# Causal latent attention: the mask added by a TensorE product before the exponential, in place of GpSimd selects and keep-busy products

## The chip, the cores and the metric

One Trainium2 chip, one core of it. The metric is device time of one execution in microseconds (us), the median of several runs. TensorE is the matrix engine (PE in the profile, PEld its weight loads), VectorE is DVE, ScalarE is ACT, GpSimd is POOL, SyncE is SP.

## The reference, cut to what matters

The whole kernel is a stack of four layers of gated attention and feed-forward blocks on x of shape (8, 256, 128). The changed part is the causal latent attention of layer 1. Per batch b of 8, with 16 heads of width 8 and T = 256 rows:

```
x = rmsnorm(x)
q = (x @ Wq.T);  latent = layernorm(x @ Wdkv.T)
k = latent @ Wuk.T;  v = latent @ Wuv.T
q, k = apply_rope(q), apply_rope(k)
scores = einsum('bhqd,bhkd->bhqk', q, k) / sqrt(8)
scores = where(causal, scores, -inf)
attn = softmax(scores);  out = einsum('bhqk,bhkd->bhqd', attn, v) @ Wo.T
```

`causal` lets query i see the keys 0 to i.

## The kernel before, in words

All of the stage is in `latent_attention_layer` (line 1622). Each engine runs its own program; all walk the same list of **slots** (`slots(4)`, line 347): 16 slots n = 0 to 15 per batch b, one head per slot, from b = -4 to the batch after the last. What a slot holds besides its head is written out by hand as `if n == ... and alive(b + ...)`. So in one slot the engines work on the head of batch b, on the maxima of a head six slots ahead (`scored`, line 353), on the output of batch b - 1 and on the preparation of batches b + 1 to b + 4. Engines meet by semaphores only, and each engine keeps the order of its program: a wait holds everything behind it.

The main chain of a head: TensorE computes the scores twice, once with queries on the partitions for the maxima (line 1901) and once transposed, keys on the partitions (line 1907). Both are products over 32 rows, on row strips `head_strip(m)` and `head_strip(n)` (line 488), two per kind. VectorE takes the masked maxima of the first (line 1799, two passes a head, each with a short read of the accumulator), ScalarE takes the exponential of the second into the tile of probabilities (line 1839). Both kinds of scores have two PSUM banks, so TensorE may be two heads ahead of either engine, no more. The maxima of a whole batch go, split in three bf16 parts, into extra columns of the queries (`place_max`, lines 1781 to 1791, four short VectorE operations, each waiting for the one before), and the queries are turned again (line 1976), so that the score product subtracts the maximum by itself.

The exponentials of keys later than the query are not wanted. Before, GpSimd sets them to zero afterwards: `hide_later` (line 1716) runs two `affine_select` (line 1722) for every four heads, four slots after their group began, and signals `masked`. The mix of the probabilities with the values (`mix_group`, lines 1912 to 1926, 16 products) waits for that and stands in slots 9, 13, 1 and 5.

Other steps of a batch, by slot on TensorE: 0 turn of the normalised rows (1939) and of half 0 of the output of batch b - 1 (1990, `pe_turn_out_half`, products of line 565); 3 query and latent projection (1947) and turn of the queries (1954); 7 turn of the keys; 9 turn of half 1 of the output; 10 turn of the latent rows (1965); 12 turn of the attention output (1970) and of the queries with their maxima; 13 key/value product (1980); 15 output product (1986). In slots 1, 2, 10 and 11 two further products each, `pe_keep_busy` (line 585, product of line 588: 128 rows, 512 columns, bf16), write to a bank that nothing reads. VectorE: sum into the result in slot 0 (1805), which frees the output bank for the mix of slot 1; normalisation of an output half in slots 1 and 10 (`dve_normalise_half`, lines 575 and 580); row statistics 2, latent statistics 4, copy of the turned queries 5 (480), latent rows 8, placing of the maxima 9, copy 13 (485). ScalarE: expansions 0 and 2 (1832), copies 1, 6, 8, 11, copy of the output 13 (1874), of keys and values 14 (1867, 1870), of an output half 6 and 14 (557). GpSimd: selects 0, 4, 8, 12; low parts 1 and 3; latent scale 5; rows 6 (1666); rotation of the queries 9 and of the keys 14 (1704 to 1708); root mean square 13.

## Time and profile before

| | us |
|---|---|
| median of 3 runs | 1438.57 (1437.09 to 1443.74) |
| the profiled execution, its own time | 1453.79 |
| its span | 1452.0 |
| TensorE, VectorE, ScalarE, GpSimd busy | 1257.5, 828.2, 640.0, 615.5 |
| the attention of the change, from its first instruction to its last | 515.3 to 704.8 |
| granted TensorE clock, mean over the span | 0.912 of full |

The table is read from the head of the page and the timeline. The profiled execution is some 1% longer than the median. "Idle before" in a row is the time in which the engine had nothing to do, and behind the arrow stands what ended it.

### The profile page before, as it was taken

How to read it: one execution, taken by the hardware profiler on the slowest of the kernel's cores; microseconds unless marked ns; L12 is line 12 of the kernel's file. 1: busy time of each engine (PE TensorE's matmuls, PEld its weight loads, DVE VectorE, ACT ScalarE, POOL GpSimd, SP SyncE). 2: the span in 40 equal slices, each digit the busy share in tenths (PEclk: the TensorE clock that was granted, in tenths of full speed). 3: DMA queues.
4: the chain of work that ended last, by engine and by line, in shares of the span. 5: the costliest groups of instructions: out<-in, count | busy, mean ns of one | idle time of the engine just before them, and what ended most of it. 6: DMA issues, size and time to landing. Idle time of an engine off the chain costs nothing.

```text
span 1452.0 us, 26160 instructions
## 1 busy us (share of the span) xinstructions
PE 1257.5 (87%) x9483; PEld 864.9 (60%) x9483; DVE 828.2 (57%) x2599; ACT 640.0 (44%) x1310; POOL 615.5 (42%) x1162
## 2 busy tenths in 40 slices
PE   6999844799999938888799989988989899989897
PEld 3444323357778723444588944444877576878786
DVE  5568487455544237886266667873555443355554
ACT  1457634355554323666322227765223464232322
POOL 4234174675763276884334434533233783000000
PEclk9999956599999955999899969998999999899999
DMA  4400000000000000000000000001200000000001
GB/s 130 138 1 2 2 1 0 1 1 1 2 1 1 1 0 1 2 2 2 1 0 0 1 1 2 2 2 33 97 0 1 1 1 1 1 1 0 0 0 30
DMA packets 15337, 16.85 MB, mean 12 GB/s; under 512 B 6403, under 2 KB 12565, under 8 KB 14583
## 3 DMA queue, kind: packets, MB, share of 16 engines
q1 hardware_dynamic: 15222, 15.34, 3.4%
q8 instruction: 70, 1.15, 0.3%
q14 instruction: 45, 0.36, 0.1%
HBM read 14.28 MB, written 1.05 MB: 11 GB/s over the span
## 4 chain that ended last, share of the span: by engine, by line
PE 35%; DVE 6%; POOL 5%; issue 3%; ACT 2%; DVEq 0%; POOLq 0%; ACTq 0%
PE banks L3056 6%; PE banks L2446 4%; PE banks L3064 4%; PE banks L2194 3%; PE banks L2472 2%; PE banks L2810 2%; PE banks L2184 2%; PE banks L511 1%; PE banks L2781 1%; PE banks L550 1%; PE banks L2795 1%; PE banks L2857 1%; DVE x_resident L2137 1%; DVE f_hiddenT L2997 1%; PE banks L2455 1%
## 5 line engine op out<-in xcount | busy, mean ns | idle before, releaser
L525 DVE TENSOR_REDUCE x_minus_max<-banks 128x2 f32<-128x512 f32 x256 | 170.3, 687 | 68.7 <-PE banks L511 67.3
L533 ACT ACTIVATE x_probs<-banks 128x512 f32<-128x512 f32 x256 | 151.5, 600 | 102.8 <-PE banks L517 101.8
L511 PE MATMUL banks<-x_kT,x_qT 32*128 32x256 bf16 x512 | 108.3, 317 | 18.7 <-DVE x_minus_max L525 10.3
L3056 PE MATMUL banks<-xnT,w_f_w 128*128 128x256 f32 x512 | 119.8, 379 | 0.0
L517 PE MATMUL banks<-x_qT,x_kT 32*128 32x256 bf16 x512 | 102.8, 301 | 2.4 <-ACT x_probs L533 1.9
L3056 PEld LDWEIGHTS banks<-xnT,w_f_w 128*128 128x128 f32 x512 | 93.0, 190 | 10.3
L3031 ACT ACTIVATE f_gate<-banks 128x512 f32<-128x512 f32 x64 | 38.2, 597 | 127.6 <-PE banks L3056 127.6
L1799 DVE CUSTOM_DVE_ANT_0 f_masked_scores<-banks,hide_later_keys 128x128 f32<-128x128 f32 (+1 forms) x256 | 77.6, 352 | 28.1 <-PE banks L1901 27.1
L2997 DVE TENSOR_TENSOR f_hiddenT<-banks,f_gate 128x512 f32<-128x512 f32 x64 | 44.0, 689 | 70.8 <-ACT f_gate L3031 70.4
L511 PEld LDWEIGHTS banks<-x_kT,x_qT 32*128 32x128 bf16 x512 | 28.9, 96 | 90.8 <-DVE x_minus_max L525 50.6
L3064 PE MATMUL banks<-w_f_w,f_hiddenT 128*128 128x128 f32 x512 | 69.6, 279 | 15.1 <-DVE f_hiddenT L2997 15.1
L1839 ACT ACTIVATE f_probs<-banks 128x384 f32<-128x384 f32 x128 | 61.5, 497 | 47.5 <-PE banks L1907 47.0
L550 PE MATMUL banks<-x_probs,x_v_with_ones 128*32 128x256 f32 x1024 | 78.9, 433 | 0.4 <-ACT x_probs L533 0.4
L3064 PEld LDWEIGHTS banks<-w_f_w,f_hiddenT 128*128 128x128 f32 x512 | 64.9, 191 | 21.3 <-DVE f_hiddenT L2997 19.5
L1215 DVE TENSOR_REDUCE x_minus_max<-banks 128x2 f32<-128x512 f32 x64 | 43.3, 687 | 58.9 <-PE banks L1472 58.9
L222 POOL TENSOR_TENSOR ln_var_eps<-ln_mean_var,eps_1e 128x2 f32<-128x2 f32 x8 | 1.6, 197 | 173.6 <-DVE ln_mean_var L202 173.6
L2194 PE MATMUL banks<-w_f_w,m_hiddenT 128*128 128x128 f32 x512 | 63.7, 281 | 4.0 <-DVE m_hiddenT L2125 4.0
L2155 ACT ACTIVATE m_hiddenT<-banks,w_f_b 128x256 f32<-128x256 f32 x64 | 26.9, 471 | 89.2 <-PE banks L2184 89.2
L2194 PEld LDWEIGHTS banks<-w_f_w,m_hiddenT 128*128 128x128 f32 x512 | 60.8, 196 | 6.7 <-ACT m_hiddenT L2155 6.6
L1502 PEld LDWEIGHTS banks<-x_v_with_one,x_probs 128*128 128x128 f32 x512 | 60.3, 192 | 5.6 <-issue 5.6
L2184 PE MATMUL banks<-m_rowsT,w_f_w 128*128 128x256 f32 x256 | 61.7, 391 | 0.0
L1502 PE MATMUL banks<-x_v_with_one,x_probs 128*128 128x65 f32 x512 | 61.0, 273 | 0.0
(514 smaller groups left out, 3109.9 us busy)
## 6 DMA issues: line engine op xcount, KB each, us to landing
w_f_w<-in_f_w SPq DMA_DIRECT2D x5, 1024.0 KB, 6.9
out<-x_resident SPq DMA_DIRECT2D x1, 1024.0 KB, 5.1
x_resident<-in_x SPq DMA_DIRECT2D x1, 896.0 KB, 6.4
context_rows<-in_ctx SPq DMA_DIRECT2D x1, 768.0 KB, 4.9
contextT<-in_ctxT SPq DMA_DIRECT2D x1, 672.0 KB, 8.7
w_f_wg<-in_f_wg SPq DMA_DIRECT2D x1, 544.0 KB, 4.9
w_f_wu<-in_f_wu SPq DMA_DIRECT2D x1, 544.0 KB, 5.8
w_f_wd<-in_f_wd SPq DMA_DIRECT2D x1, 512.0 KB, 6.4
```

Of the source, the lines that this page charges most:

```text
L511: mm = nc.tensor.matmul(K.PS[:, SMAX0 + m % 2, t * S:(t + 1) * S], h["qT"][r, c % 3, g, t * P:(t + 1) * P], h["kT"][r, c % 3, g, :], start ...
L517: mm = nc.tensor.matmul(K.PS[:, ST0 + n % 2, t * S:(t + 1) * S], h["kT"][r, b % 3, g, t * P:(t + 1) * P], h["qT"][r, b % 3, g, :], start=T ...
L525: K.nc.vector.tensor_reduce(h["nm"][:, b % 2, :, n], K.PS[:, SMAX0 + n % 2, :].rearrange("p (t n) -> p t n", t=T), AX_X, ALU.max, negate=T ...
L533: K.nc.scalar.activation(h["p"][:, n % (2 * HG)], K.PS[:, ST0 + n % 2, :], ACT.Exp).then_inc(s["p"].sem, 1)
L550: mm = nc.tensor.matmul(K.PS[E * j:E * (j + 1), OUT0 + g // 2, (g % 2) * S:(g % 2 + 1) * S], h["ve"][:, b % 3, kt * H + n, :], h["p"][:, n ...
L1502: mm = nc.tensor.matmul(K.PS[:, OUT0 + t, at:at + V1], p[:, (2 * c + j) % 4, kt * S + t * P:kt * S + (t + 1) * P], ve[:, b % 2, kt, 2 * c ...
L1799: ins = nc.vector.tensor_tensor_reduce(unused[:, m % 2, t, 0:w], K.PS[:, SMAX0 + m % 2, t * P:t * P + w], hide[:, t, 0:w], -1.0, -HIDE, AL ...
L1839: nc.scalar.activation(h["p"][:, (b * H + n) % PROBS], K.PS[:, ST0 + n % 2, 0:WIDE], ACT.Exp).then_inc(s["p"].sem, 1)
L2184: mm = nc.tensor.matmul(K.PS[:, 2 * (e % 2) + c // 2, (c % 2) * S:(c % 2 + 1) * S], W["f1_w1"][:, (e * CE1 + c) * P:(e * CE1 + c + 1) * P] ...
L2194: mm = nc.tensor.matmul(K.PS[:, OUT0 + e % 2, t * D:(t + 1) * D], hT[:, e % 2, c, t * P:(t + 1) * P], W["f1_w2"][:, (e * CE1 + c) * D:(e * ...
L3056: mm = nc.tensor.matmul(K.PS[:, 2 * (e % 2) + k, c * S:(c + 1) * S], W[name][:, e * HE3 + c * P:e * HE3 + (c + 1) * P], K.norm["xnT"][:, u ...
L3064: mm = nc.tensor.matmul(K.PS[:, OUT0 + e % 2, t * D:(t + 1) * D], hT[:, e % 2, c, t * P:(t + 1) * P], W["f3_w2"][:, (e * CE3 + c) * D:(e * ...
```

## The change

The mask becomes a summand of the scores. For each head a product of the constant tile `hidden` (-1e30 where the key is later than the query, 0 elsewhere, in bf16, 128 x 128) with the identity, broadcast to both diagonal blocks, opens the accumulation of the score bank (256 columns, all 128 rows), and the two score products of line 1907 add to it. The exponential gives zero there by itself. GpSimd's selects and their semaphore are gone, and so are the eight keep-busy products of a batch. The mix waits for the exponentials. Several steps change slot: half 0 of the output turn from 0 to 2 and its normalisation from 1 to 3, turn of the queries 3 to 4, half 1 of the output turn 9 to 8 and its normalisation 10 to 9, attention output turn 12 to 11 and its copy 13 to 12, key/value product 13 to 14 with its copies and the rotation of the keys 14 to 15. `place_max` is a generator, whose four operations are spread: at the ends of slots 9 and 10, and between the two passes of the maxima in slots 10 and 11.

```diff
 def causal_mixed_at(b, n):
-    i = b * H + n - MASKED_SLOT
+    i = b * H + n - MIXED_LATE
...
@@ gpsimd
-                def hide_later(b, g):
-                    first = (b * G + g) % 3 * HG
-                    pool.wait_ge(s["p"].sem, s["p"].after(b, HG * (g + 1)))
-                    for kt in range(T):
-                        d = h["p"][:, first:first + HG, kt * S:kt * S + P]
-                        ins = nc.gpsimd.affine_select(d, d, pattern=[[0, HG], [1, P]], compare_op=ALU.is_ge, fill=0.0, base=0, channel_multiplier=-1)
-                    ins.then_inc(s["masked"].sem, 1)
...
-                    if n == 14 and alive(b + 3):
+                    if n == 15 and alive(b + 3):
                         rotate(b + 3, 1, s["k_read"], "ks", W["f1_rope"][:].rearrange("p (a t e) -> p a t e", a=2, t=T), s["rolled_k"])
@@ vector
+                nc.vector.tensor_copy(hidden[:], hide[:, 0, 0:P]).then_inc(ready.sem, 1)
...
                     nc.vector.tensor_copy(qe[:, :, :, 24], m).then_inc(steps.sem, 1)
-                    dve.wait_ge(steps.sem, steps.next())
+                    got = steps.next()
+                    yield
+                    dve.wait_ge(steps.sem, got)
                     nc.vector.tensor_tensor(h["nr"][:], m, qe[:, :, :, 24], ALU.subtract).then_inc(steps.sem, 1)
...
                         for t in range(T):
+                            if placing is not None and (n, t) in ((10, 1), (11, 1)):
+                                next(placing)
...
-                    if n == 1 and alive(b - 1):
+                    if n == 3 and alive(b - 1):
                         dve_normalise_half(K, dve, steps, s, h, b - 1, 0, None)
...
-                    if n == 9 and alive(b + 1):
-                        place_max(b + 1)
-                    if n == 10 and alive(b - 1):
+                    if n == 9 and alive(b - 1):
                         dve_normalise_half(K, dve, steps, s, h, b - 1, 1, None)
+                    if n == 9:
+                        placing = place_max(b + 1) if alive(b + 1) else None
+                    if n in (9, 10) and placing is not None:
+                        next(placing)
@@ tensor
+                    if alive(b):
+                        nc.tensor.matmul(K.PS[:, ST0 + n % 2, :].rearrange("p (t n) -> p t n", t=T)[:, :, 0:P], hidden[:],
+                                         K.identb[:].unsqueeze(1).broadcast_to([P, T, P]), start=True, stop=False, skip_group_check=True)
...
                             mm = nc.tensor.matmul(K.PS[:, ST0 + n % 2, t * S:t * S + (T - t) * P], h["kT"][r, b % 3, g, t * P:(t + 1) * P],
-                                                  h["qT"][r, b % 3, g, t * P:S], start=True, stop=True)
+                                                  h["qT"][r, b % 3, g, t * P:S], start=False, stop=True, skip_group_check=True)
...
                 def mix_group(b, g):
-                    pe.wait_ge(s["masked"].sem, s["masked"].after(b, g + 1))
+                    pe.wait_ge(s["p"].sem, s["p"].after(b, HG * (g + 1)))
...
-                    if n == 13 and alive(c):
+                    if n == 14 and alive(c):
                         pe.wait_ge(s["latT"].sem, s["latT"].after(c))
...
-                    if n == 0 and alive(b - 1):
+                    if n == 2 and alive(b - 1):
                         pe_turn_out_half(K, pe, s, h, b - 1, 0)
-                    if alive(b):
-                        last, before = min(c, B - 1), min(c - 1, B - 1)
-                        if n in (1, 2):
-                            pe.wait_ge(s["v"].sem, s["v"].after(before))
-                            pe.wait_ge(s["k_read"].sem, s["k_read"].after(before))
-                            pe_keep_busy(K, h, b, MISC)
-                            pe_keep_busy(K, h, b, MISC)
-                        if n in (10, 11):
-                            pe.wait_ge(s["lat"].sem, s["lat"].after(last))
-                            pe.wait_ge(s["q_read"].sem, s["q_read"].after(last))
-                            pe_keep_busy(K, h, b, MISC + 1)
-                            pe_keep_busy(K, h, b, MISC + 1)
```

The other slot changes are of the same form.

## Rows read from the trace of the kernel before

**Rows 1.** The page: TensorE's granted clock in 40 equal slices of the span

```profile
PEclk9999956599999955999899969998999999899999
```

**Rows 2.** Windows: length, PE PEld DVE ACT POOL busy (count), clock, DMA, GB/s

```profile
564.20:584.32 20.12, 17.65 (x144) 8.25 (x145) 14.94 (x84) 11.72 (x27) 14.35 (x30) 0.65 0.01 2
602.24:620.16 17.92, 15.75 (x188) 8.48 (x188) 15.17 (x86) 12.18 (x30) 15.75 (x33) 1.00 0.01 1
638.10:656.66 18.56, 16.67 (x185) 8.89 (x184) 14.70 (x82) 12.02 (x29) 12.06 (x25) 0.91 0.01 2
656.66:671.08 14.42, 13.25 (x176) 6.77 (x176) 12.14 (x72) 10.37 (x24) 7.55 (x14) 1.00 0.01 2
671.08:685.30 14.22, 12.13 (x146) 5.89 (x145) 9.18 (x51) 8.56 (x21) 4.90 (x8) 1.00 0.01 1
685.30:699.00 13.70, 11.70 (x126) 5.47 (x127) 1.66 (x6) 8.68 (x20) 5.34 (x9) 1.00 0.00 1
```

**Rows 3.** Timeline of TensorE, slot 13 to slot 3: start, us, engine, line, operation

```profile
615.86 0.23 PE L1901 MATMUL banks<-f_kT,f_qT 32*128 32x128 bf16 x1
...
616.92 1.13 PE L1980 MATMUL banks<-f_w_k_v,f_latT 128*128 128x256 f32 x4
...
617.98 0.23 PE L1901 MATMUL banks<-f_kT,f_qT 32*128 32x128 bf16 x1
...
618.00 0.22 PE L1901 MATMUL banks<-f_kT,f_qT 32*128 32x128 bf16 x1
...
619.05 0.09 PEld L1901 LDWEIGHTS banks<-f_kT,f_qT 32*128 32x128 bf16 x1 [0.27 <-DVE f_minus_max L1799]
...
619.32 0.44 PE L1939 MATMUL banks<-identity,y_resident 128*128 128x128 f32 x2
...
619.97 0.65 PE L565 MATMUL banks<-identity,f_outT 128*128 128x128 f32 x4 [0.21 <-ACT f_outT L557]
...
620.56 0.22 PE L1901 MATMUL banks<-f_kT,f_qT 32*128 32x128 bf16 x1
...
622.16 0.22 PE L1901 MATMUL banks<-f_kT,f_qT 32*128 32x128 bf16 x1
...
622.43 0.60 PE L588 MATMUL banks<-f_kT 128*128 128x512 bf16 x2
...
622.96 0.23 PE L1901 MATMUL banks<-f_kT,f_qT 32*128 32x128 bf16 x1
```

**Rows 4.** Timeline of VectorE and GpSimd, slots 9 to 11, and VectorE's wait in slot 4

```profile
612.07 0.35 DVE L1785 CAST f_q_expanded<-f_minus_max 128x32 bf16<-128x32 f32 x1
...
612.65 1.23 POOL L1722 TENSOR_SCALAR_AFFINE_SELECT f_probs<-f_probs 128x512 f32<-128x512 f32 x2
...
612.70 0.68 DVE L1789 CAST f_q_expanded<-f_minus_max_rest 128x32 bf16<-128x32 f32 x1
...
613.86 0.28 DVE L1799 CUSTOM_DVE_ANT_0 f_masked_scores<-banks,hide_later_keys 128x128 f32<-128x128 f32 x1
...
614.42 0.25 DVE L575 RECIPROCAL f_inverse_sums<-banks 128x16 f32<-128x16 f32 x1
...
614.70 0.29 DVE L580 TENSOR_TENSOR f_attention_out<-banks,f_inverse_sums 128x128 f32<-128x128 f32 x1
...
624.90 0.29 DVE L1799 CUSTOM_DVE_ANT_0 f_masked_scores<-banks,hide_later_keys 128x128 f32<-128x128 f32 x1 [0.52 <-PE banks L1901]
```

**Rows 5.** Timeline: the same cast beside a rotation step, and alone in batch 5

```profile
648.61 0.72 POOL L1708 TENSOR_TENSOR f_q_rows<-f_turned_a,f_turned_b 128x256 f32<-128x256 f32 x1
648.63 0.79 DVE L1789 CAST f_q_expanded<-f_minus_max_rest 128x32 bf16<-128x32 f32 x1
...
665.62 0.24 DVE L1789 CAST f_q_expanded<-f_minus_max_rest 128x32 bf16<-128x32 f32 x1
```

**Rows 6.** A window with the clock down in batch 4; timeline: the last mix

```profile
648.00:649.00 1.00, 1.00 (x8) 0.72 (x4) 0.93 (x3) 0.00 (x0) 0.92 (x3) 0.50 0.00 0
...
699.84 0.59 PEld L1923 LDWEIGHTS banks<-f_probs,f_v_with_ones 128*32 128x32 f32 x16 [0.50 <-POOL f_probs L1722]
```

More of the change, by code:

```diff
@@ L1602 @@
 LAT = 64
-MASKED_SLOT = 9
-def masked_at(b, n):
-    i = b * H + n - HG
-    if i % HG == 0 and alive(i // H):
-        return i // H, (i % H) // HG
-    return None
+MIXED_LATE = 9
 def causal_mixed_at(b, n):
-    i = b * H + n - MASKED_SLOT
+    i = b * H + n - MIXED_LATE
     if i % HG == 0 and alive(i // H):
@@ L1628, in latent_attention_layer @@
         s[extra] = K.rising("signal_" + extra, 1)
-    s["masked"] = K.rising("signal_masked", G)
     WIDE = S + P
@@ L1645, in latent_attention_layer @@
         hide = K.hide_q
-        ready = K.once("layer_setup_step", 2)
+        hidden = sb("hide_later_bf16", [P, P], BF16)
+        ready = K.once("layer_setup_step", 3)
         cleared = K.once("heads_values_cleared", 1)
@@ L1727, in _ @@
                 for b, n in slots(4):
-                    group = masked_at(b, n)
-                    if group:
-                        hide_later(*group)
                     if n == 1 and alive(b + 2):
@@ L1785, in place_max @@
                     nc.vector.tensor_copy(qe[:, :, :, 24], m).then_inc(steps.sem, 1)
-                    dve.wait_ge(steps.sem, steps.next())
+                    got = steps.next()
+                    yield
+                    dve.wait_ge(steps.sem, got)
                     nc.vector.tensor_tensor(h["nr"][:], m, qe[:, :, :, 24], ALU.subtract).then_inc(steps.sem, 1)
-                    dve.wait_ge(steps.sem, steps.next())
+                    got = steps.next()
+                    yield
+                    dve.wait_ge(steps.sem, got)
                     nc.vector.tensor_copy(qe[:, :, :, 25], h["nr"][:]).then_inc(steps.sem, 1)
-                    dve.wait_ge(steps.sem, steps.next())
+                    got = steps.next()
+                    yield
+                    dve.wait_ge(steps.sem, got)
                     nc.vector.tensor_tensor(qe[:, :, :, 26], h["nr"][:], qe[:, :, :, 25], ALU.subtract).then_inc(s["qm"].sem, 1)
+                    yield
+                placing = None
                 for b, n in slots(4):
                     c, m = scored(b, n)
+                    if placing is not None and n in (10, 11) and not alive(c):
+                        next(placing)
                     if alive(c):
@@ L1815, in _ @@
                         latent_rows(b + 3)
-                    if n == 9 and alive(b + 1):
-                        place_max(b + 1)
-                    if n == 10 and alive(b - 1):
+                    if n == 9 and alive(b - 1):
                         dve_normalise_half(K, dve, steps, s, h, b - 1, 1, None)
+                    if n == 9:
+                        placing = place_max(b + 1) if alive(b + 1) else None
+                    if n in (9, 10) and placing is not None:
+                        next(placing)
                     if n == 13 and alive(b + 1):
@@ L1863, in _ @@
                             .then_inc(s["latT"].sem, 1)
-                    if n == 14 and alive(c):
+                    if n == 15 and alive(c):
                         kv = K.PS[:, MISC, :].rearrange("p (t n) -> p t n", t=T)
@@ L1871, in _ @@
                                              kv[:, :, D:2 * D].rearrange("p t (h e) -> p t h e", e=DH), ACT.Copy).then_inc(s["v"].sem, 1)
-                    if n == 13 and alive(b - 1):
+                    if n == 12 and alive(b - 1):
                         act.wait_ge(s["woT_ps"].sem, s["woT_ps"].after(b - 1))
@@ L1949, in _ @@
                         mm.then_inc(s["q_ps"].sem, 1)
-                    if n == 3 and alive(b + 2):
+                    if n == 4 and alive(b + 2):
                         pe.wait_ge(s["v"].sem, s["v"].after(b + 2))
@@ L1957, in _ @@
                         pe_turn_k(K, pe, s, h, b + 2)
-                    if n == 9 and alive(b - 1):
+                    if n == 8 and alive(b - 1):
                         pe_turn_out_half(K, pe, s, h, b - 1, 1)
@@ L1966, in _ @@
                         mm.then_inc(s["latT_ps"].sem, 1)
-                    if n == 12 and alive(b - 1):
+                    if n == 11 and alive(b - 1):
                         pe.wait_ge(s["o"].sem, s["o"].after(b - 1))
```

## The prediction

> **What bounds the kernel now.** The page comes first, for where the stage lies and what clock TensorE was granted: the changed attention takes about 190 of 1452 us (slices 15 to 20 of the page), and its first third ran at half clock [rows 1]. Next, the busy time by batch, in windows for batches 0, 2, 4, 5, 6 and 7 [rows 2]. While batches 1 to 3 run, the later ones are also being prepared, and a batch takes 17.92 us; TensorE is busy 15.75 of them, VectorE 15.17, ScalarE 12.18 and GpSimd 15.75. No engine is full, so a chain across engines sets the period. The last three batches have less and less beside them (14.42, 14.22, 13.70 us), and the first one ran mostly at the low clock (20.12 us at a mean 0.65).
>
> Then the timeline of TensorE and of VectorE through one batch shows the two legs of that chain. **Leg 1**, slot 13 to slot 2, 615.86 to 622.16, 6.30 us, is TensorE's queue: mixes, the key/value product, the output product, and 0.54 us of keep-busy products in slot 1 [rows 3]. **Leg 2**, slot 2 to the next slot 13, the other 11.62 us, is VectorE's: its masked maxima, copies, and the placing of the maxima. In slot 9 the placing took 1.79 us (612.07 to 613.86) and all score products queued behind it [rows 4]. ScalarE waits in both legs, but for TensorE.
>
> All sums are against the profiled execution, 1453.79 us. It is 1.1% above the median of 1438.57, so I carry differences over, not totals. About 0.5%, 7.2 us here, is what a measurement of this kernel can tell from no change.
>
> **Keep-busy products out.** A pair takes a score slot from 0.27 to 0.80 us (622.16, 622.43, 622.96) [rows 3]. Eight of them in a batch are four pairs at 0.54: 2.16 us less on TensorE, one pair of it in leg 1. In leg 2 they stand where VectorE is late anyway, and I count nothing: VectorE's steps cover them.
>
> **Mask product in.** The trace has none. A keep-busy product is its like: same rows, same 128 weight columns, bf16, 0.27 us for 512 columns. Halving it all for 256 columns gives the lower bound, 0.135; the whole 0.27 is the upper one. With 0.21 us of streaming at 2.4 GHz in the 0.27, the fixed part is 0.06, so 0.11 + 0.06 = 0.16 to 0.17; I take 0.16. Sixteen make 2.6 us: TensorE's sum grows by 0.4 a batch instead of shrinking. There is a second cost. Now two consecutive score groups lie on different 32-row strips and run at once: 617.98 and 618.00 both start within 0.02 us [rows 3]. A product over all 128 rows between them ends that; each such pair costs about 0.27 us more, one of them in leg 1. So leg 1 pays 5 x 0.16 + 0.27 = 1.07 us, and leg 2 pays the mask once, 0.16, since VectorE is the late one there.
>
> The Trainium skill (TensorE: Matmul & The Clock Gate, "The mechanism" of row and column tiling) speaks against this edit too: weight loads overlap running products only where the row groups differ, so the mask's load would be exposed. The paired starts agree with its positive half; by a fully exposed load, priced at the 0.27 bound, the sum below would be about 4 us worse.
>
> **Slots spread.** Half 0 of the output turn leaves slot 0 for slot 2. That takes 0.59 us (619.97 to 620.56) out of leg 1, and with the key/value product now in slot 14 the two waits of the leg, 0.25 before 619.06 and some 0.4 before 619.97, can close [rows 3]. What is late next: the mix of slot 1 needs a bank that VectorE frees with its sum of slot 0, and nothing stands between any more; I price that at 0.4 us (the wait of the same kind that closes, no row nearer). Leg 1: 6.30 - 0.54 - 0.59 - 0.62 + 1.07 + 0.40 = 6.0 us.
>
> In leg 2 VectorE stood 0.52 us before 624.90 for scores behind the projection and the query turn; with the turn in slot 4 this closes. The first normalisation moves into the leg, +0.57 (614.42 to 614.99) [rows 4]. Placing in four pieces between the maxima drops the semaphore gaps and GpSimd's hold. Here the cast of 612.70 took 0.68 us beside a select that began 612.65; alone it is 0.24 (665.62) [rows 4, 5]. Four such short operations without a hold, at about 0.25 us, make 1.0: 0.8 less. Leg 2: 11.62 - 0.52 + 0.57 - 0.80 + 0.16 = 11.0.
>
> But with the selects gone GpSimd reaches its query rotation 1.2 us earlier, so the rotation now lies on the placing. A cast beside a rotation step took 0.79 us (648.63, the step at 648.61) [rows 5], 0.55 more than alone. No hit bounds it at 0, a hit on each later step at about 1.0; the nearest rows show one. I take +0.6: leg 2 is 11.6.
>
> The Trainium skill (SBUF — State Buffer, "SBUF: two separate sides") says that GpSimd and a VectorE operation with two SBUF inputs, or in a two-port mode, exclude each other for a whole instruction. The rows show this for a cast with one input, so I go by them; with the two subtractions alone held, the extra would be of the same size.
>
> **Selects out.** Eight a batch leave GpSimd, at 1.23 us for two [rows 4]. Mixes come nine slots after their heads, before and after, so nothing waited for them but the last mix, behind its select at 699.84: -0.3 us [rows 6]. Value and key copies one slot later: 0, covered by the two slots until the expansion; at most 0.3 a batch without that cover.
>
> **The sum.** A steady batch: 6.0 + 11.6 = 17.6 against 17.92, three times -0.3 = -1.0 us. Batch 4 has no row step ahead of the rotation, so no hold, and it had lost 0.64 us to a spell of low clock (18.56, 0.91): about 17.2, -1.3. Batch 5: TensorE busy 13.25 - 2.16 + 2.6 + 0.3 = 14.0 of 14.42: -0.3. Batches 6 and 7: 12.13 and 11.70 become 12.6 and 12.1, no VectorE leg: -0.6 each. Tail -0.3, lead-in -0.5 (one placing, less one small cast). Batch 0: its mean of 0.65 says the clock rose after 70%, near slot 11, with keep-busy products just ahead. Without these I expect it at slot 14, behind mix and key/value product. Slots 11 to 14 hold about 4.4 us of TensorE work at full clock (four score groups with masks at 0.43, a query turn at 0.54, mix and key/value product at 1.85), which half clock at most doubles; part of that lies beside VectorE's steps. I take +3, less 0.4 for its placing. Total: -1.0 - 1.3 - 0.3 - 1.2 - 0.3 - 0.5 + 2.6 = -2.0. That is 1451.8 for the profile and 1436.6 for the median.
>
> **Rivals.** *Faster* (0.25): the rotation misses the placing, and sixteen spread mask products lift the clock in batch 0 as early as before or some slots earlier. Steady batches take 17.0 (-2.7), batch 4 -1.5, batch 0 -2.5, the rest -2.3: -9.0, 1429.6. For it: a hold needs an exact overlap. Against: nothing dense came earlier. *Slower* (0.15): in slots 10 to 12 nothing dense is left, and the clock falls there in every batch, to rise only behind the key/value product. That happened once between mixes of slots 5 and 9, at 648 [rows 6], and cost 0.64 with keep-busy products right behind; without them mix and key/value product (1.85 us from 616.13, where the scores begun at 615.86 end, to 617.98) run at half speed, +1.5, masks and scores +0.7: 2.2 a batch. It decides from five batches up; in seven, +15.4 - 2.0 gives 1452. Against: masks now stand in every gap. *The change doesn't relieve anything* (0.08): placing is held as long as before and every wait only moves, steady batches stay at 17.9: +1.5, 1440. The forecast keeps 0.52.
>
> **Numbers.** My own case with its bounds (mask 0.135 to 0.27, hold 0 to 1.0, batch 0 from 0 to +6) spans 1431 to 1443; with most of both outer rivals the range is 1427 to 1448. Chances: faster 0.27 (the faster rival and a little of my case), same 0.53, slower 0.20 (the slower rival and the dear ends of mine).
>
> **What would show it.** Right: mask products near 0.16 us start to start, no pair of score groups started at once, no wait of scores for the placing in slots 10 to 12, batches near 17.6, clock of batch 0 rising at slot 13 or 14, casts of 0.5 to 0.8 us beside a rotation. Wrong: a batch below 17.0 or above 18.3, the clock below full in more than two of batches 1 to 7, or a change outside the stage.

## The result, and the profile after

The changed kernel took 1429.69 us in the median of 9 runs (1426.93 to 1434.64), the kernel before 1439.48 beside it (9 runs). The ratio is 0.9942, with a 95% interval of 0.992 to 0.9964: 8.4 us faster by the ratio, where the forecast was 2 us and "no change". The profiled execution took 1428.87 us, with a span of 1427.1. Two of the profiled executions, that of the kernel before (1453.79 us) and that of mask_free further down, were slow ones and lost 14 and some 38 us ahead of the stage (it began at 516.1 and 539.8 us, in before_again at 502.2), so of these two only the stage and what lies behind it are read.

The first view is the page's line of TensorE's granted clock over the whole span, in 40 slices.

```profile
PEclk9999855799999856999899969998999999999999
```

Against [rows 1] the stage again begins at half clock. A difference also stands far behind it: slice 35 is at 9 where it was at 8. The windows by batch answer to [rows 2]: first the lead-in, then batches 0 to 7, then the tail. The columns are the same.

```profile
499.36:546.49 47.13, 28.72 (x126) 15.48 (x127) 26.31 (x143) 11.08 (x24) 34.58 (x76) 0.50 0.00 1
546.49:566.89 20.40, 19.20 (x150) 9.30 (x151) 14.13 (x81) 11.59 (x27) 10.28 (x25) 0.67 0.01 2
566.89:584.13 17.24, 16.53 (x195) 9.31 (x194) 14.46 (x85) 12.44 (x30) 11.05 (x25) 1.00 0.01 2
584.13:601.84 17.71, 16.58 (x195) 9.37 (x195) 14.85 (x86) 12.43 (x29) 10.95 (x25) 1.00 0.01 2
601.84:619.55 17.71, 16.59 (x195) 9.38 (x195) 14.85 (x86) 12.43 (x29) 10.95 (x25) 1.00 0.01 1
619.55:636.54 16.99, 16.38 (x195) 9.31 (x194) 13.74 (x82) 12.31 (x29) 7.35 (x17) 1.00 0.01 2
636.54:651.40 14.86, 14.14 (x182) 7.64 (x181) 12.48 (x75) 10.54 (x23) 3.43 (x7) 1.00 0.01 2
651.40:665.85 14.45, 13.32 (x155) 6.85 (x152) 9.14 (x51) 8.80 (x20) 0.00 (x0) 1.00 0.01 2
665.85:678.36 12.51, 12.31 (x125) 6.17 (x123) 1.31 (x5) 8.18 (x20) 0.00 (x0) 1.00 0.00 1
678.36:685.87 7.51, 4.26 (x48) 2.50 (x47) 1.95 (x6) 1.48 (x4) 0.00 (x0) 1.00 0.00 0
```

Batch 7 ends here with the start of its last exponential, where the last window of [rows 2] runs 1.0 us past it. Cut in the same way, batch 7 of the kernel before is

```profile
685.30:698.00 12.70, 10.86 (x116) 4.89 (x114) 1.31 (x5) 8.18 (x19) 4.90 (x8) 1.00 0.00 1
```

A steady batch went from 17.92 to 17.71 us. Work moved between engines: GpSimd does 4.8 us less in it (15.75 to 10.95), TensorE 0.84 more (15.75 to 16.59). Batch 4 gained most, 18.56 to 16.99; batches 5 and 6 lost 0.44 and 0.23.

TensorE's timeline through slots 1 to 5 shows the mask products (L1894), the scores behind them, and one wait.

```profile
601.98 0.27 PE L1894 MATMUL banks<-identity_bf,f_hide_later_bf 128*128 128x256 bf16 x1
602.18 0.22 PE L1899 MATMUL banks<-f_kT,f_qT 32*128 32x128 bf16 x1
...
602.93 0.86 PE L1921 MATMUL banks<-f_probs,f_v_with_ones 128*32 128x256 f32 x16 [0.41 <-DVE y_resident L1798]
603.72 0.28 PE L1894 MATMUL banks<-identity_bf,f_hide_later_bf 128*128 128x256 bf16 x1
603.94 0.22 PE L1899 MATMUL banks<-f_kT,f_qT 32*128 32x128 bf16 x1
...
608.12 0.28 PE L1894 MATMUL banks<-identity_bf,f_hide_later_bf 128*128 128x256 bf16 x1
608.33 0.22 PE L1899 MATMUL banks<-f_kT,f_qT 32*128 32x128 bf16 x1
...
608.60 0.28 PE L1894 MATMUL banks<-identity_bf,f_hide_later_bf 128*128 128x256 bf16 x1
608.82 0.23 PE L1899 MATMUL banks<-f_kT,f_qT 32*128 32x128 bf16 x1
```

From the start of a mask product to the start of its scores it is 0.20 to 0.22 us. A score slot costs 0.48 (608.12 to 608.60) where it cost 0.27 [rows 3], and two groups that start together are not to be found there. The third mix waits 0.41 us for the residual's add. One more wait, of 0.45 us, stands further on, before the turn of the queries with their maxima, for the last operation of the placing.

The timeline of VectorE and GpSimd through slots 9 to 12 answers to [rows 4]: the placing (L1766, L1770, L1774, L1778) between the maxima, beside the query rotation (L1696 to L1700).

```profile
612.21 0.72 POOL L1696 TENSOR_TENSOR f_turned_a<-f_raw_rows,f_rope_for_q 128x256 f32<-128x256 f32 x1
...
612.41 0.62 DVE L1766 CAST f_q_expanded<-f_minus_max 128x32 bf16<-128x32 f32 x1
...
613.10 0.27 DVE L1770 TENSOR_TENSOR f_minus_max_rest<-f_minus_max,f_q_expanded 128x32 f32<-128x32 f32 x1
...
613.63 0.23 DVE L1774 CAST f_q_expanded<-f_minus_max_rest 128x32 bf16<-128x32 f32 x1
...
613.73 0.73 POOL L1700 TENSOR_TENSOR f_q_rows<-f_turned_a,f_turned_b 128x256 f32<-128x256 f32 x1
...
613.92 0.69 DVE L1778 TENSOR_TENSOR f_q_expanded<-f_minus_max_rest,f_q_expanded 128x32 bf16<-128x32 f32 x1
```

So the foreseen hold is there: the two operations that meet a 0.72 us rotation step take 0.62 and 0.69 us, the other two 0.27 and 0.23.

Last, the same windows for batch 0, cut where the clock changes.

```profile
546.49:553.30 6.81, 6.81 (x40) 3.41 (x40) 4.42 (x29) 3.79 (x9) 3.29 (x9) 0.50 0.01 4
553.30:560.60 7.30, 6.10 (x72) 2.98 (x73) 6.98 (x39) 5.42 (x12) 6.59 (x15) 0.97 0.00 1
560.60:566.89 6.29, 6.29 (x42) 2.91 (x42) 2.73 (x14) 2.39 (x7) 0.40 (x2) 0.50 0.00 0
```

The clock rose at 553, near slot 6 and well before the forecast's slot 14, and fell again for the last four slots.

### The profile page after: what moved, and what is told of

Same layout as the page of the kernel before. It is cut to its first block, busy times and chain, and to the rows that moved or that the text cites. A ratio compares the mean times of both kernels' runs of the same rounds, so it can differ in the third digit from the quotient of the medians.

```text
span 1427.1 us, 26181 instructions
## 1 busy us (share of the span) xinstructions
PE 1240.7 (87%) x9536; PEld 863.7 (61%) x9547; DVE 823.8 (58%) x2600; ACT 640.3 (45%) x1310; POOL 575.4 (40%) x1098
## 4 chain that ended last, share of the span: by engine, by line
PE 36%; DVE 6%; POOL 5%; issue 3%; ACT 2%; DVEq 0%; POOLq 0%; ACTq 0%
PE banks L3040 6%; PE banks L2430 4%; PE banks L3048 4%; PE banks L2178 3%; PE banks L2456 2%; PE banks L2794 2%; PE banks L2168 2%; PE banks L2765 1%; PE banks L511 1%; PE banks L550 1%; PE banks L2779 1%; PE banks L2841 1%; DVE x_resident L2121 1%; DVE f_hiddenT L2981 1%; PE banks L2439 1%
## 5 line engine op out<-in xcount | busy, mean ns | idle before, releaser
L511 PE MATMUL banks<-x_kT,x_qT 32*128 32x256 bf16 x512 | 102.1, 300 | 22.2 <-DVE x_minus_max L525 11.1
L517 PE MATMUL banks<-x_qT,x_kT 32*128 32x256 bf16 x512 | 97.7, 286 | 3.0 <-ACT x_probs L533 2.4
L3015 ACT ACTIVATE f_gate<-banks 128x512 f32<-128x512 f32 x64 | 38.2, 597 | 127.6 <-PE banks L3040 127.6
L550 PE MATMUL banks<-x_probs,x_v_with_ones 128*32 128x256 f32 x1024 | 72.9, 406 | 0.4 <-ACT x_probs L533 0.4
```

The source lines that it names most:

```text
L511: mm = nc.tensor.matmul(K.PS[:, SMAX0 + m % 2, t * S:(t + 1) * S], h["qT"][r, c % 3, g, t * P:(t + 1) * P], h["kT"][r, c % 3, g, :], start ...
L517: mm = nc.tensor.matmul(K.PS[:, ST0 + n % 2, t * S:(t + 1) * S], h["kT"][r, b % 3, g, t * P:(t + 1) * P], h["qT"][r, b % 3, g, :], start=T ...
L550: mm = nc.tensor.matmul(K.PS[E * j:E * (j + 1), OUT0 + g // 2, (g % 2) * S:(g % 2 + 1) * S], h["ve"][:, b % 3, kt * H + n, :], h["p"][:, n ...
```

## The experiments

The theory under test (order): a steady batch's time is set by two legs, and the change shortens them by spreading the placing and moving tasks, while the mask product is a cost, and GpSimd's hold and the residual's add are what it left behind. The first rival (clock) puts the gain in keep-busy products that go and in the clock of TensorE; the second (mask) in the selects that leave GpSimd. Here are all runs. "Batches 0+1" is the time from the first exponential to the first residual add, "steady" the time between the next adds. "Stage" is from the clearing of the latent rows to the next layer's first squares. "Behind" is the rest of the span, where all kernels have the same code. The last four columns come from the one profiled execution of each.

| run | median us | ratio to before, 95% | steady | batches 0+1 | stage | behind |
|---|---|---|---|---|---|---|
| before | 1439.48 | | 17.92 | 37.9 | 189.0 | 746.8 |
| after | 1429.69 | 0.9942 [0.992, 0.9964] | 17.71 | 38.2 | 185.7 | 741.2 |
| before_again | 1439.17 | 0.9979 [0.9943, 1.0014] | 17.90 | 38.2 | 190.0 | 746.8 |
| after_again | 1430.94 | 0.9913 [0.9873, 0.9953] | 17.72 | 35.1 | 182.2 | 743.4 |
| place_whole | 1438.6 | 1.0004 [0.9962, 1.0046] | 20.1 | 39.7 | 193.8 | 743.4 |
| hold_off | 1431.55 | 0.9919 [0.9881, 0.9958] | 16.98 | 37.4 | 182.7 | 744.2 |
| mask_in | 1447.86 | 1.0117 [1.0083, 1.0151] | 18.68 | 39.9 | 199.9 | 742.7 |
| busy_out | 1446.15 | 1.009 [1.0056, 1.0124] | 19.2 to 17.5 | 40.5 | 198.5 | 747.9 |
| busy_back | 1441.84 | 1.0052 [1.002, 1.0083] | 18.70 | 36.6 | 192.8 | 748.1 |
| mask_free | 1429.8 | 0.999 [0.9953, 1.0026] | 16.98 | 35.9 | 182.1 | 746.6 |
| busy_first | 1437.89 | 0.9998 [0.9967, 1.0029] | 17.73 | 38.2 | 185.8 | 751.2 |
| y_first | 1433.31 | 0.9986 [0.9959, 1.0014] | 17.24 | 34.2 | 179.9 | 745.3 |
| hold_y | 1426.7 | 0.9943 [0.9918, 0.9969] | 16.51 | 36.4 | 179.9 | 743.5 |
| all_three | 1428.12 | 0.9929 [0.9898, 0.9959] | 16.51 | 34.6 | 178.0 | 754.4 |

The four runs from before_again to hold_off share 33 runs of the kernel before (median 1441.68), the next four 27 (1433.71), the last four 35 (1438.85). These three sets ran on three different chips, and the kernel after stands in the first set alone: beside the runs of the last two sets there is no neighbour to show what it takes on their chips.

**The two kernels once more.** No edit.

> The kernel before, unchanged, profiled once more, so that its stages can be set beside those of the changed kernel. In the first pair of profiles the attention stage took 189.8 us before and 186.5 after, while the whole differs by 8 to 10 us in the timed runs. Order theory (the gain is made in the stage, by queues that wait less): this profile shows a stage of 192 to 196 us, so that the stage alone holds the 8 us. Clock theory (the stage gives 3 us, the rest is which stretches ran at the low clock): the stage is again 189 to 190.5, and the other 5 us lie outside it, in stretches whose granted clock differs.

> The changed kernel, unchanged, profiled once more. Both theories: a ratio of 0.992 to 0.997, steady batches of 17.7 us and a stage of 186 to 187.5 us if nothing in it hangs on the clock's phase; the clock theory allows 184 to 192, with the difference in batch 0 (20.4 us in the first profile) and in windows below full clock.

Both came out as in the first comparison, 8.2 us apart by their medians. The kernel before repeated its stage (189.0 and 190.0 us) and the part behind it (746.8 twice), as the clock theory had said. But inside the stage the two profiles of the same changed kernel differ by 3.5 us, and 3.0 of these lie in batches 0 and 1, 38.2 and 35.1 us: here the clock was full when batch 0 began, and only one short spell followed. The steady batches repeat to 0.01.

**place_whole: the placing in one piece.**

```
 if n == 9:
-    placing = place_max(b + 1) if alive(b + 1) else None
-if n in (9, 10) and placing is not None:
-    next(placing)
+    for _ in place_max(b + 1) if alive(b + 1) else (): pass
```

with the other two calls of `next(placing)` taken out.

> The changed kernel with the placing of the maxima in one piece at the end of slot 9 again, all else as changed. Order theory, by my step for it: the placing stands in VectorE's leg with its semaphore gaps, 0.5 to 0.8 us more in each of seven batches, so 4 to 5 us slower than the changed kernel, ratio to before 0.997 to 1.000. Rival (GpSimd's rotation holds the pieces wherever they stand, so spreading them is worth nothing): steady batches stay at 17.7 and the ratio at 0.993 to 0.995.

The whole gain was gone: ratio 1.0004, and the two batches behind the first residual add took 20.10 and 20.14 us. TensorE's timeline at slot 11, and two windows of that batch (the columns as before):

```profile
599.04 0.28 PE L1889 MATMUL banks<-identity_bf,f_hide_later_bf 128*128 128x256 bf16 x1 [1.45 <-DVE f_minus_max L1788]
...
600.46 1.51 PE L1916 MATMUL banks<-f_probs,f_v_with_ones 128*32 128x256 f32 x16
```

```profile
600.30:603.70 3.40, 3.40 (x28) 1.69 (x25) 1.89 (x9) 1.53 (x4) 0.00 (x0) 0.52 0.02 5
585.74:600.30 14.56, 12.50 (x154) 7.07 (x154) 13.04 (x72) 9.81 (x23) 10.85 (x24) 1.00 0.01 2
```

TensorE waits 1.45 us for the maxima (its weight load 1.68, against 0.29 in the kernel after, at 613.76). Then its clock falls for 3.4 us, and the mix takes 1.51 us in place of 0.86. Such a wait stands in each of batches 1 to 3. In batches 2 and 3 the clock fell behind it, and they were 2.4 us longer than in the kernel after; in batch 1 it held, and the batch was 0.5 us longer (17.74 and 17.24, from exponential to exponential). So the wait by itself costs about 0.5 us, and the larger part, 1.9, comes with the fall of the clock. Batch 0 has a wait too, of 1.90 us, but the clock had fallen at 559.5, before that wait was over, and in the kernel after it fell at 560.2 with no such wait, so nothing is read from it. The forecast had priced the spreading at 0.8, and the expectation at 0.5 to 0.8.

**busy_out: the kernel before without its keep-busy products.** The block of `if alive(b):` with the four pairs of `pe_keep_busy` is taken out.

> The kernel before with the keep-busy products left out and all else as before. Order theory: 0.54 us less in leg 1 of a steady batch, 17.9 to 17.4, and 1 us less in each of the last three, where TensorE is the late engine: 4 to 6 us faster, 0.996 to 0.997, as far as the clock holds. Clock theory: the clock rises later in batch 0 and falls between the mixes of slots 9 and 13 in several batches, each time 0.6 to 2.2 us: 1.000 to 1.010.

It was 0.9% slower, against the order theory and inside the range of the clock theory: the products did earn their place in the old order. The same views of this kernel, first TensorE's timeline in slots 11 to 13, then windows:

```profile
600.45 0.23 PE L1901 MATMUL banks<-f_kT,f_qT 32*128 32x128 bf16 x1 [1.45 <-DVE f_minus_max L1799]
...
602.03 1.36 PE L1923 MATMUL banks<-f_probs,f_v_with_ones 128*32 128x256 f32 x16
603.32 2.08 PE L1980 MATMUL banks<-f_w_k_v,f_latT 128*128 128x256 f32 x4
```

```profile
588.57:602.00 13.43, 9.86 (x140) 5.60 (x138) 11.95 (x68) 9.54 (x22) 12.24 (x26) 1.00 0.01 2
602.00:605.40 3.40, 3.40 (x27) 1.83 (x28) 1.25 (x5) 0.77 (x2) 2.48 (x7) 0.53 0.00 0
```

This is the mechanism of the forecast's *slower* rival, in another kernel than the changed one: the same 1.45 us wait behind a placing in one piece, then a 3.4 us spell at half clock under the mix and the key/value product (2.08 us where [rows 3] has 1.13). Batch 0 stayed at half clock to its end (21.41 us at a mean 0.50), and the last batches fell too, 30.7 us in a row. It is not so in every batch. Batch 1 had a wait of 1.31 us and such a spell behind it, batches 4 and 5 one of 1.34 and one of 1.53 without a spell, and in batch 3 the clock fell at 615.9, near slot 7, where no product had waited for more than 0.75 us. In the changed kernel no product waits for more than 0.5 us in slots 10 to 12 of batches 1 to 4, and no spell there; place_whole speaks for the one being the reason of the other.

**busy_back: the kernel after with the keep-busy products in all batches.** The same block put back behind the last task of TensorE's loop.

> The changed kernel with the eight keep-busy products of a batch back in slots 1, 2, 10 and 11. Order theory: TensorE's queue is 16.6 of 17.7 us full, so 2.16 us more a batch show nearly whole, steady batches 19 to 19.7, last three 1.5 to 2 longer: 12 to 16 us slower than the changed kernel, ratio 1.002 to 1.006. Clock theory: batch 0 keeps the clock that it lost at slot 12 in the changed kernel and wins 2 to 3 us back, and the ratio stays below 1.001.

Steady batches grew to 18.70 us, less than the 19 to 19.7 expected, with TensorE busy 17.88 of them, and the four behind them to 18.7, 16.5, 15.3 and 14.7. Batches 0 and 1 took 36.6, in the middle of what the order without the products gives; the clock rose at 549.3 us, near slot 3 of batch 0, and stayed up to the end of the stage. The ratio of 1.0052 is 1.4% above the 0.9913 of after_again, which ran on another chip. In the new order the products cost a full microsecond a batch, since TensorE has become the fullest engine.

**mask_in: the kernel before with the mask product for the selects alone.** Keep-busy products, slots and placing as before.

> The kernel before with one part of the change alone: the mask product ahead of the score products in place of GpSimd's selects. Keep-busy products, slots and placing as before. Order theory: sixteen mask products at the 0.21 us that the changed kernel shows from the start of one to the start of its scores, on TensorE's queue, half of them where VectorE is late anyway: steady batches 17.9 to 19 or 19.5 us, less 0.4 for a placing that no select holds; 6 to 10 us slower than before, ratio 1.004 to 1.007. Rival (the low clock of batch 0 is the larger term and spread dense products lift it early): batch 0 shrinks from 20.1 to 18 or less and the ratio is 0.998 to 1.003.

1.2% slower, more than the 0.4 to 0.7% expected: TensorE is busy 18.04 us of an 18.68 us batch, and batch 0 did not shrink (20.99 us). So exchanging the selects for the mask product brings nothing by itself, and mask product and keep-busy products together overfill TensorE. What the selects alone cost is not shown: no run keeps them in the new order, and none moves the tasks to other slots and does nothing else.

**mask_free: the kernel after without the mask product.** This kernel doesn't leave future keys out of the scores that are exponentiated; the rest is computed.

```
-nc.tensor.matmul(K.PS[:, ST0 + n % 2, :]..., hidden[:], K.identb[:]..., start=True, stop=False, ...)
-    h["qT"][r, b % 3, g, t * P:S], start=False, stop=True, skip_group_check=True)
+    h["qT"][r, b % 3, g, t * P:S], start=True, stop=True)
```

> The changed kernel without the mask product, with the score products opening their bank themselves as before; future keys are then not left out of the softmax. It prices the mask product. By the 0.21 us from start to start, five of them in leg 1, and two pairs of score groups that can start together again: steady batches 17.7 to 16.3 or 16.6, ratio 0.985 to 0.989, if the clock holds. Rival (without dense products in every slot the clock falls in slots 6 to 8 and 10 to 12): windows at half clock in most batches, batches 17.5 and more, ratio 0.994 or above.

Steady batches of 16.98: the sixteen products cost 0.73 us net a batch, not their gross 16 x 0.21 = 3.4, as most of it lies where TensorE otherwise waits for VectorE. That is less gain than the theory asked (16.3 to 16.6), and the rival, with batches of 17.5 and more, missed too. In batches 1 to 3 TensorE waited up to 1.03 us at a time, before the turn of the queries with their maxima, and no spell followed. The clock did fall around the last batch, which took 14.85 us from one residual add to the next where the kernel after takes 12.98. The ratio, 0.999, shows no gain over the kernel before.

**hold_off: the query rotation waits until the maxima are placed.**

```
 if n == 9 and alive(b + 3):
+    if alive(b + 1):
+        pool.wait_ge(s["qm"].sem, s["qm"].after(b + 1))
     rotate(b + 3, 0, ...
```

> The changed kernel with one wait more: GpSimd begins the rotation of the queries only when the maxima of the same slots are placed, so no placing operation runs beside a rotation step. My step says the hold costs 0.6 us a batch (two of the four operations took 0.62 and 0.69 us beside rotation steps in the profile of the changed kernel, 0.24 and 0.30 alone): steady batches 17.7 to 17.0 or 17.1, three or four of them, 2 to 4 us faster than the changed kernel, ratio 0.990 to 0.993. Rival (TensorE's queue is full by now, 16.6 of 17.7 us, and the hold is hidden behind it): steady batches 17.5 to 17.7, no difference. Third: the rotation comes too late for the expansion in slot 0 and ScalarE waits there, batches 17.9 or more.

VectorE's timeline of one steady batch, the placing without a neighbour:

```profile
610.50 0.23 DVE L1768 CAST f_q_expanded<-f_minus_max 128x32 bf16<-128x32 f32 x1
...
610.93 0.21 DVE L1772 TENSOR_TENSOR f_minus_max_rest<-f_minus_max,f_q_expanded 128x32 f32<-128x32 f32 x1
...
611.40 0.24 DVE L1776 CAST f_q_expanded<-f_minus_max_rest 128x32 bf16<-128x32 f32 x1
...
611.70 0.30 DVE L1780 TENSOR_TENSOR f_q_expanded<-f_minus_max_rest,f_q_expanded 128x32 bf16<-128x32 f32 x1
```

0.98 us in sum in place of 1.81, and the batch went from 17.72 to 16.98, as expected. The hold is 0.83 us on VectorE and 0.74 on the path. Yet the kernel did not get faster than after_again, run beside it (1431.55 and 1430.94), where 2 to 4 us were expected. These are its batch 0 and a steady batch:

```profile
546.06:566.82 20.76, 20.76 (x153) 9.89 (x155) 13.69 (x83) 11.52 (x27) 10.30 (x25) 0.57 0.01 2
583.48:600.46 16.98, 16.37 (x198) 9.36 (x194) 14.17 (x86) 12.31 (x29) 11.00 (x25) 1.00 0.01 2
```

Batch 0 ran at a mean clock of 0.57, and batches 0 and 1 gave back 2.3 us where the steady ones had gained 0.74 each.

**y_first: the residual's add ahead of the maxima of slot 0**, on VectorE.

```
+if n == 0 and alive(b - 2):
+    y1 = ...   # the three lines of the add, moved up
 if alive(c):
     dve.wait_ge(s["smax_ps"].sem, s["smax_ps"].after(c, m + 1))
```

> The kernel after, with the residual's add on VectorE ahead of the maxima of its slot 0 in place of behind them. My theory (the 0.41 us in which the third mix waits for that add stand on the path of TensorE's leg): the wait of the L1921 mix for L1798 goes, the maxima of slot 0 come 0.3 us later, which TensorE asks for only two slots later; a steady batch takes 17.3 to 17.5 us in place of 17.7, the late ones 0.2 to 0.4 less each; the stage 180 to 183 us, the kernel 1.5 to 3 us less than the kernel after (ratio to the kernel before 0.988 to 0.994). Rival (the wait is slack of a leg that VectorE sets behind it, the maxima only change places with the add): the wait goes and comes back in front of a later product of scores, a steady batch stays at 17.7, and the ratio is that of the kernel after, 0.991 to 0.996.

The wait is gone. The same mix in TensorE's timeline now follows its scores directly:

```profile
600.22 0.21 PE L1905 MATMUL banks<-f_qT,f_kT 32*128 32x128 bf16 x1
600.36 0.86 PE L1921 MATMUL banks<-f_probs,f_v_with_ones 128*32 128x256 f32 x16
```

A steady batch takes 17.24 us, 0.48 less, and batch 5 (14.29 from one residual add to the next) 0.74 less. The stage is the 180 us expected. The whole kernel is not: 0.9986, outside what both theories had given.

**hold_y: both edits.**

> The kernel after, with both: the q rotation of GpSimd waits until the maxima are placed, and the residual's add is ahead of the maxima of slot 0. My theory: the two lie on different legs of the cycle (slots 9 to 12 and slots 0 to 2), so they add up; steady batches take 16.6 to 16.8 us (16.98 with the rotation's wait alone, and 0.2 to 0.4 less by the add), the stage 179 to 182 us, the kernel 2 to 4 us less than the kernel after, ratio to the kernel before 0.987 to 0.992. Rival (at 16.98 all batches stand at the same new bound, the chain of scores and exponentials or TensorE's clock in batch 0 takes the rest back, as it took the rotation's 0.7 us back): steady batches stay at 16.98, batch 0 stays longer at the half clock, and the ratio is 0.991 to 0.995.

16.51 us: 0.74 and 0.48 make 1.22, and 1.21 was found. What TensorE waited for in one steady batch (us in total, times, longest), after and in this kernel:

```profile
PE banks L266 <- DVE f_q_expanded L1778: 0.5, 1, 0.5
PE banks L1921 <- DVE y_resident L1798: 0.4, 1, 0.4
PE banks L565 <- ACT f_outT L557: 0.2, 1, 0.2
```

```profile
PE banks L565 <- ACT f_outT L557: 0.2, 1, 0.2
```

TensorE is busy 16.31 of 16.51 us, so here it is the bound. The kernel is the fastest of the job by its median, 1426.7. Whether it beats the kernel after is not shown: its ratio, 0.9943, is that of the kernel after in the first comparison and in the range of the rival, and the two were not run side by side. hold_y and y_first have the same stage time, 179.9, and medians 6.6 us apart, so something else moves the total.

**busy_first and all_three: the keep-busy products in batch 0 alone** (`if b == 0:` in place of `if alive(b):`), on the kernel after and on hold_y.

> The kernel after, with the keep-busy products of the kernel before in slots 1, 2, 10 and 11 of batch 0 alone (8 calls). My theory (the keep-busy products earn their place only where TensorE is otherwise too idle to hold its clock, and that is batch 0): batch 0 runs at the full clock from about slot 6 on, as with the keep-busy products in all batches, the batches 1 to 7 stay at 17.7, 17.0, 15.0, 13.5 and 13.0 us; batch 0 takes 17.9 to 18.6 us where the two profiles of the kernel after gave 20.4 and about 17.4. So the stage takes 182 to 184 us, and the kernel 0 to 2 us less than the kernel after in this job's neighbours (ratio to the kernel before 0.990 to 0.995). Rival (the clock of batch 0 is a matter of phase that such products do not set): the half-clock stretch behind slot 11 of batch 0 stands there in this profile too, and the ratio is that of the kernel after or above it, 0.994 to 0.997.

> The kernel after, with all three: keep-busy products in batch 0 alone, GpSimd's q rotation behind the placing, the residual's add ahead of the maxima of slot 0. My theory: batch 0 keeps its clock (18 us or less) and the steady batches take 16.6 to 17.0 us, so the stage takes 178 to 181 us, the kernel 3 to 6 us less than the kernel after, ratio to the kernel before 0.985 to 0.990. Rival (what the stage gains in its batches comes back in its batch 0 and behind the stage by the phase of TensorE's clock, whatever is done): the stage takes 182 us or more, or the part behind it 746 us in place of 743, and the ratio is 0.991 to 0.995.

In busy_first batch 0 took 20.85 us at a mean clock of 0.67, no better than without them; in all_three 18.86 at 0.83. So my theory that these products set the time at which the clock of batch 0 rises falls, and the ratio of busy_first, 0.9998, is outside what both theories had given. That they keep it up once it has risen is not excluded: in busy_back, busy_first and all_three it did not fall again before the end of the stage, while without them it fell once more in batch 0 in after, after_again, place_whole, mask_free and y_first, though not in hold_off and hold_y. Over all kernels with the new order batches 0 and 1, less two steady ones, range from -0.8 (busy_back) to 3.5 us (hold_off), and the two profiles of the kernel after alone span 3.0 of that. all_three has the shortest stage of all, 178.0 us, and the longest part behind it, 754.4, as its rival said.

**Where the rest of the time lies.** The part behind the stage has the same instructions in every kernel, and took 741 to 754 us. The two profiles taken beside each other make it plain. In both, the first window starts at the end of the stage; the second holds the same stretch of code (88 and 86 product records); the third is the rest of the span. First the kernel before, then the kernel after:

```profile
692.26:1227.26 535.00, 491.67 (x3608) 351.26 (x3609) 305.10 (x832) 225.32 (x507) 233.89 (x427) 0.93 0.03 10
1227.26:1242.26 15.00, 14.29 (x88) 12.42 (x88) 4.32 (x24) 5.18 (x12) 0.00 (x0) 0.76 0.00 1
1242.26:1439.10 196.84, 175.07 (x1060) 157.35 (x1059) 106.79 (x370) 61.08 (x99) 6.25 (x14) 0.99 0.02 6
```

```profile
681.74:1216.74 535.00, 491.59 (x3610) 351.51 (x3610) 304.98 (x832) 225.72 (x508) 234.02 (x427) 0.93 0.03 10
1216.74:1228.20 11.46, 10.75 (x86) 9.57 (x86) 4.18 (x23) 4.82 (x11) 0.00 (x0) 0.99 0.01 1
1228.20:1425.10 196.90, 175.15 (x1061) 157.43 (x1059) 106.77 (x371) 61.08 (x99) 6.25 (x14) 0.99 0.02 6
```

In the first 535 us the two did the same work, the last 197 are equal to a tenth, and the whole 3.5 us lie in one place, where TensorE's clock stood at a mean 0.76 in the one and 0.99 in the other. Both profiles of the kernel before have this spell, so has busy_first. All fourteen profiles agree with this, to some 1 us: the more of the part behind the stage ran at half clock, the longer it is. It took 741.2 us with 75.0 at half clock (after), 743.4 with 81.2 (after_again, place_whole and hold_y alike), 746.8 with 88 (the kernel before, twice), 751.2 with 102.3 (busy_first) and 754.4 with 112.6 (all_three). What decides how much that is was not settled.

## Why the prediction was right in its range and wrong in its size

By its own steps:

- **Steady batch, 17.6: right.** 17.71 was measured, in legs of 6.22 us (the mask products of slot 13 at 615.21 and of slot 2 at 621.43) and 11.49, where 6.0 and 11.6 were forecast. Part of the 0.2 by which leg 1 is longer is a misreading: the two waits that were to close are 0.27 and 0.21 in [rows 3], 0.48 together and not 0.62. Batches 1 to 3 took 17.24, 17.71 and 17.71, together 1.1 us less than before, against the forecast's 1.0.
- **Mask product, 0.16: too low,** 0.20 to 0.22, inside its bounds, and TensorE's sum grew by 0.84 us a batch in place of 0.4. The rule of the Trainium skill (TensorE: Matmul & The Clock Gate, "The mechanism") that loads overlap running products only where the row groups differ is agreed with by the starts: mask and score share row groups and start 0.21 us apart, and the paired starts of [rows 3] are gone. The rows do not prove it, since the scores at 608.33 begin 0.07 us before the modelled end of their mask product. What the 0.21 is made of no run here shows.
- **GpSimd's hold, +0.6: right,** 0.74 by hold_off. It hit two operations instead of one. One is a cast with a single SBUF input, as in [rows 5]. The rule of the Trainium skill (SBUF — State Buffer, "SBUF: two separate sides") names operations with two inputs or in a two-port mode; the subtraction fits it, and in which mode the cast ran no row shows.
- **New wait for the residual's bank, 0.40: right,** 0.41. The sum left it out of batch 5, where it is 0.68 us (TensorE busy 14.14, as forecast at 14.0, plus this wait, is 14.82 of the 14.86). Batch 5 became 0.44 longer in place of 0.3 shorter.
- **Batch 4, -1.3: right,** -1.57.
- **Batches 6 and 7, -0.6 each: wrong,** +0.23 and -0.2. The step took their length from TensorE's sum beside other waits. For batch 7 the window of [rows 2] also held 1.0 us of the tail. Batch 7 is now TensorE's alone (12.31 busy of 12.51), and its work grew by 1.45 us: the masks, with the pairs they part, cost more than the keep-busy products gave.
- **Tail, -0.3: wrong,** +0.35. The select's wait went, but the last mix now follows the output turn of slot 2, and a mix ahead of it waits 0.61 us for the residual's add.
- **Lead-in, -0.5: mis-sized.** It is 48.07 and 48.81 us in the two profiles of the kernel before, 46.32 and 45.87 after, measured from the clearing of the latent rows to the first exponential. Nearly all of it runs at half clock (the clock rose 0.9 us before its end in after_again, behind it in the other three). place_whole, with the spreading undone, has 47.14, so the spreading is 0.8 to 1.3 of the gain; what the rest is stays open.
- **Batch 0, +2.6: wrong.** The step had the clock rise at slot 14 without keep-busy products. It rose near slot 6 in one profile of the kernel after and ahead of slot 0 in the other; batches 0 and 1 were 0.3 us longer in one pair of profiles and 3.0 shorter in the other. This was the largest term of the sum, and it rested on one clock reading. Its 4.4 us of work is also 4.1 by its own parts.
- **Placing, -0.8: near as a wait, but the clock behind it was left out.** Against the new order with the placing left whole it saves 0.5 us where the clock holds and 2.4 where it falls. The steady batch came out near all the same, most likely because the kernel before had no such fall to lose: its keep-busy products stand in these slots, and busy_out, without them, has the spell in batches 1 and 2.
- **Nothing outside the stage: wrong,** and on the forecast's own list of what would show it wrong. The profile pairs give -5.6 and -3.5 us behind the stage. Ahead of it the second pair gives -2.7; the first can't be read there.

Added up, the stage gave 3.3 us in the first pair of profiles and 7.8 in the second (2.0 forecast), and the part behind it 5.6 and 3.5: 8.9 and 11.3 in sum, where the medians differ by 9.8 and 8.2. The second pair differs by 14.0 in all, with the 2.7 ahead of the stage; one execution is not the median. That the result lies in the range is owed to the room left for the *faster* rival: my own case with its bounds reached down to 1431 only. The *faster* rival had the total (1429.6) but not the mechanism: its rotation was to miss the placing, and it didn't. Its other half, a clock in batch 0 that rises earlier, did occur. *Doesn't relieve anything* is refuted by place_whole.

What stays open: why the granted clock behind the stage, and in batch 0, falls for longer in some kernels and executions than in others. One or two profiles of a kernel can't tell an effect of the code from one of the phase in which the clock meets it. That the kernel after keeps its gain over 19 runs in two jobs says that its total is lower, not how much of it the stage gives and how much the clock in the rest.

## What to carry to other kernels

Short dependent operations on an engine whose results the next engine awaits are worth spreading between its other work: the wait can cost twice, once itself (0.5 us here) and once in a clock that falls behind it (1.9 more, in two batches of three). Before a task is moved off a busy-looking engine, check which engine is full after the move; here GpSimd lost 4.8 us of work a batch, TensorE gained 0.84 and became the fullest engine, and the mask product costs 0.73 us of each steady batch. Whether the new order would do better with the selects left on GpSimd was not tried. Expect a stage's gain to come back from the total with several microseconds of noise from the clock, and compare stage times in the profile beside the medians.

## What was not expected of the hardware

- A wait of 1.45 us on TensorE was followed within 2 us by 3.4 us at half clock in batches 2 and 3 of place_whole and batch 2 of busy_out, and a wait of 1.44 in batch 1 of place_whole was not, nor one of 1.53 in batch 5 of busy_out. Behind the waits of the kernel after, of 0.68 us at most, there was none in batches 1 to 7, nor behind the 1.03 us waits of mask_free in its batches 1 to 3.
- The same short stretch of the same code took 15.00 us at a mean clock of 0.76 in one kernel and 11.46 at 0.99 in the other, 535 us behind the last instruction in which they differ. In the kernel before, two executions had the same spells of half clock behind the stage, nine of them, each at the same distance from the stage's end to 0.1 us.
